# Far sums one group later on TensorE, and GpSimd's gathers with one wait a group

## The reference

```python
h = maximum(layernorm(x), 0)
# per edge: 8 radial functions of the distance -> two layers of 64 with silu -> 128 weights
weight = silu(silu(rbf @ fc_w1 / sqrt(8)) @ fc_w2 / 8) @ fc_w3 / 8
gs, gv = lin1(h)[src]                      # 32 scalars and 32 vectors of each edge's source node
msg_s = [w00 * gs * sh0, w11 * (gv . sh1) / sqrt(3)]
msg_v = [w01 * gs x sh1, w10 * gv * sh0]
agg = segment_sum(msg, dst) / clip(count, 1)
out = x + sc(h) + tanh(agg_s @ alpha_w) * lin2(agg)
```

## Time and profile before

| | us |
|---|---|
| median of 3 runs | 2496.71 |
| lowest, highest | 2487.68, 2497.35 |
| span of the profiled execution | 2483.8 |
| busy: TensorE, VectorE, GpSimd, ScalarE | 1811.4, 1783.0, 1578.4, 1199.1 |

### The profile page before, as it was taken

How to read it: one execution, slowest core, us unless ns; L and a number is a source line. 1 busy time by engine, 2 the same in 40 slices (tenths; PEclk the granted TensorE clock), 3 DMA queues, 4 the chain that set the end, 5 groups by cost and what they waited for, 6 DMA issues and landing times. The chain is left out here.

```text
span 2483.8 us, 34021 instructions
## 1 busy us (share of the span) xinstructions
PE 1811.4 (73%) x7969; PEld 1174.2 (47%) x7969; DVE 1783.0 (72%) x4669; ACT 1199.1 (48%) x3310; POOL 1578.4 (64%) x1624
## 2 busy tenths in 40 slices
PE   6577777787777777767677767667787776877777
PEld 6344444454444444444444434444554444544544
DVE  8577767767776777767676667767677776777777
ACT  6354545455454555444444344445444444445443
POOL 7566666666666666666666666666666666666563
PEclk9588878878888887788787878888888888888889
DMA  7322222222222222222122222222222222222222
GB/s 214 70 64 67 56 64 66 66 56 66 66 59 62 67 65 56 55 48 50 46 50 48 48 48 49 54 50 64 57 67 62 59 65 66 53 64 61 59 66 55
DMA packets 347699, 155.73 MB, mean 63 GB/s; under 512 B 237983, under 2 KB 322048, under 8 KB 347584
## 3 DMA queue, kind: packets, MB, share of 16 engines
q0 software_dynamic: 50016, 102.51, 15.7%
q1 hardware_dynamic: 296938, 51.75, 11.4%
q10 hardware_dynamic: 630, 0.29, 0.0%
HBM read 134.27 MB, written 20.15 MB: 62 GB/s over the span
## 5 line engine op out<-in xcount | busy, mean ns | idle before, releaser
L970 POOL DMA_INDIRECT lin_g<-lin_table,src_ix x1563 | 1530.0, 979 | 865.1 <-issue 441.5
L1157 ACT ACTIVATE lin_sh<-lin_g,harm 128x128 f32<-128x128 f32 x1563 | 483.8, 396 | 94.6 <-DMA lin_g<-lin_table,src_ix 87.6
L1040 PE MATMUL ps_sums<-near_sums,far_hot 128*128 128x257 f32 x520 | 208.0, 488 | 440.8 <-DVE agg L1474 206.0
L1030 PE MATMUL ps_near<-msg,onehot 128*64 128x257 f32 x3126 | 507.5, 471 | 1.2 <-DVE msg L1423 1.2
L1018 PE MATMUL ps_w<-w,h 128*128 128x256 f32 x1566 | 462.6, 440 | 28.2 <-ACT key_all L1167 18.5
L1018 PEld LDWEIGHTS ps_w<-w,h 128*128 128x128 f32 x1566 | 395.3, 272 | 135.4 <-issue 44.9
L999 PE MATMUL ps_h<-rbf,w 32*128 32x192 f32 x1044 | 277.0, 390 | 138.0 <-issue 67.1
L1415 DVE TENSOR_TENSOR msg<-lin_sh,key_all 128x576 f32<-128x576 f32 (+1 forms) x261 | 197.3, 756 | 249.9 <-ACT key_all L1167 209.5
L1167 ACT ACTIVATE key_all<-ps_w 128x768 f32<-128x768 f32 x261 | 213.5, 818 | 305.2 <-remote 188.6
L1030 PEld LDWEIGHTS ps_near<-msg,onehot 128*64 128x64 f32 x3126 | 241.3, 164 | 230.6 <-issue 175.7
L1383 DVE TENSOR_TENSOR lin_sh<-lin_g,ps_meta 128x576 f32<-128x576 f32 (+1 forms) x261 | 196.6, 753 | 212.2 <-DMA lin_g<-lin_table,src_ix 207.0
(11 more groups left out here) (175 smaller groups left out, 1655.2 us busy)
## 6 DMA issues: line engine op xcount, KB each, us to landing
lin_g<-lin_table,src_ix POOLq DMA_INDIRECT x1563
dist_in<-in_edge_weight SPq DMA_DIRECT2D x67, 96.0 KB
lin_table<-lin_out SPq DMA_DIRECT2D x24, 256.0 KB, 2.6
x_in<-in_x SPq DMA_DIRECT2D x24, 256.0 KB
skip_table<-x_in SPq DMA_DIRECT2D x24, 256.0 KB
xq<-in_x SPq DMA_DIRECT2D x23, 256.0 KB, 3.9
harm<-in_edge_attr SPq DMA_DIRECT2D x66, 48.0 KB
x_in<-skip_table SPq DMA_DIRECT2D x8, 256.0 KB
```

The costliest lines, as they stand in the source:

```text
L970: pool.indirect_dma_start(slot_tiles(s, u)[rows, t, :], None, lin_table, bass.IndirectOffsetOnAxis(ap=src_ix[rows, s.phase, u, col:col + 1 ...
L1030: mm = pe.matmul(ps_near[half * NEAR:(half + 1) * NEAR, 0:MSG + 1], onehot[:, u, t, :], msg[:, u % 2, t, :], start=(j == 0), stop=(j == PA ...
L1040: pe.matmul(ps_nodes(i), far_hot[:, u, :], near_sums[:, u % 2, :], start=True, stop=True).then_inc(sums_ready, 1)
L1157: last = act.activation(lin_sh0[:, u % 2, j, :], slot_tiles(s, u)[:, j, :], ACT.Copy, scale=harm[:, s.phase, u, harm_col(j):harm_col(j) + 1])
```

## The change

The far sum moves one group back and up: in slot g TensorE computes that of g-2, between the first and the second layer. VectorE's aggregation of g-2 stands between the product and the one-hot columns. The near sums always wait for ScalarE's copy of the sums before, since no far sum does it for them any more. `turn_early` (transposes of blocks of `agg` that are complete) waits for the aggregation of the last group of the iteration before. GpSimd keeps the wait ahead of a group's first gather and loses the two others.

```diff
@@ gather (GpSimd)
                             for k, t in enumerate(tiles):
-                                if not first and k == 2:
-                                    pool.wait_ge(h2_done, s.i * SLOTS + u)
-                                    pool.nop(nofuse=True)
-                                if not first and k == 4:
-                                    pool.wait_ge(sums_ready, s.i * SLOTS + u - SLOTS + 1)
-                                    pool.nop(nofuse=True)
@@ near_layer (TensorE)
                             pe.wait_ge(msg_ready, n + 1)
-                            if isinstance(i, int) and i == ITERS:
-                                pe.wait_ge(near_copied, n)
+                            at_least(pe, near_copied, n)
@@ turn_early (TensorE)
+                            if k == 0:
+                                pe.wait_ge(agg_ready, (EARLY0 + n) * SLOTS + 1)
@@ body (TensorE)
                                     layer1(i, u + 3)
+                                if u > 1:
+                                    segment_sum(i, u - 2)
+                                elif not isinstance(i, int) or i > 0:
+                                    segment_sum(i - 1, SLOTS - 2 + u)
                                 if not last or u + 2 <= SLOTS:
                                     layer2(i, u + 2)
                                 layer3(i, u + 1)
-                                if u > 0:
-                                    segment_sum(i, u - 1)
-                                elif not isinstance(i, int) or i > 0:
-                                    segment_sum(i - 1, SLOTS - 1)
                                 near_layer(i, u)
...
                         body(ITERS - 1, finish=True, last=True)
+                        segment_sum(ITERS - 1, SLOTS - 2)
                         segment_sum(ITERS - 1, SLOTS - 1)
@@ body (VectorE)
                             for u in range(SLOTS):
+                                if not last or u < SLOTS - 1:
+                                    products(s, u + 2)
                                 if u > 1:
                                     accumulate(i, u - 2)
                                 elif not isinstance(i, int) or i > 0:
                                     accumulate(i - 1, SLOTS - 2 + u)
                                 if not last or u < SLOTS - 1:
-                                    products(s, u + 2)
                                     columns(s, u + 2)
                                 late(s, u + 1)
```

## The result

The changed kernel takes 2580.11 us (median of 4 runs, 2561.38 to 2594.81), the kernel before 2496.42 beside it (2487.68 to 2497.35): 1.0335 times before, 95% interval 1.0285 to 1.0386. It is slower, and lies above the forecast of 2446 us and above the range of 2290 to 2570. It went as rival C had it in kind.

What follows compares the result with a forecast made beforehand. GpSimd's gathers and the gaps between them were taken as the bound: span 2483.8 - 66 (GpSimd) + 10 (TensorE) + 5 (new waits) + 0 (VectorE) = 2433 us, plus 12.9 gives 2446 us; range 2290 to 2570.

Steps and rivals of the forecast that it cites:

- rival C: GpSimd's removed pauses had kept news flowing: slower above 189 head pauses, 2542 us mostly, up to 2646; 30%.
- Step 1: GpSimd's two waits go: 154 head pauses of 1.9 us, 293 us against 359, saving 66 us.
- Step 2: TensorE's far sum moved: earlier near sums, nothing added; layers two and three later, 10 us lost (bounds 0 to 80).
- Step 3: TensorE's new waits: near sums for ScalarE's copy, zero; early transposes for the aggregation, 5 us (0 to 117).
- Step 4: VectorE's aggregation behind the product: register load hidden, up to 188 us back, or 110 us lost; taken as 0.
- A: GpSimd's wait at the head of a group rarely stops: 72 pauses left, 2258 us; 12%.
- B: Late news through ScalarE's copy, VectorE's message and the near sums sets the pace: no change, 2497 us; 13%.

Runs made afterwards that it cites:

- the memset: Kernel before without GpSimd's waits ahead of the third and fifth gather, plus a memset of 1000 values ahead of each group's fourth gather: 2515.24 us, 1.0084.
- the plain loads: Kernel before without GpSimd's waits ahead of the third and fifth gather, its gathers replaced by SyncE loading the same bytes from fixed rows: 2155.93 us, 0.8652.
- sum_late_only: Kernel before, all three GpSimd waits kept, with only TensorE's new order; VectorE's aggregation stays at the head of its slot: 2558.27 us, 1.0259.
- aggregation_late_only: Kernel before with only VectorE's aggregation moved behind the product; TensorE's order and GpSimd's three waits unchanged: 2547.57 us, 1.0074.
- gates_off_old_order: Kernel before with only GpSimd's waits ahead of the third and fifth gather removed: 2577.83 us in the one execution that counts, 1.021.

## Why the prediction was wrong

**The diagnosis was right in the main.** GpSimd's gathers and their gaps set the pace, and late completions mostly come through when it stops issuing. That was inferred from order; the memset and the plain loads show it. That a recorded matmul end is an estimate does not account for the 9 us, since such ends were right to 0.03 us with GpSimd silent. The prediction's own rows also show that news comes through beside unbroken gathers (1316.93) and that a stop of 1.71 us can leave it unsaid; it did not use this.

**Step 1, GpSimd, failed, in one term.** It forecast 154 pauses at the head and 1.9 us of excess for each, 293 us. Measured were 156 pauses with 3.21 - 0.30 = 2.91 us, 454 us: 161 above the forecast and 95 above the 359 of before. The 1.9 came from the mean of all pauses (1.66) and a little more, with the cap of 3.2 - 0.3 that "remote" pauses showed. I read those pauses as short because a gate had let news through shortly before. Pauses at the head are of another kind: after 6 gathers in a row the late news includes what the near sums themselves needed, so that TensorE is truly behind ("PE ps_near" 263.0 us in 61, longest 13.6; before 15.9 in 13; with a break added to the changed kernel 88.3 in 40). The step took the length from a state that the change removes. It said that silence would leave more unsaid, and priced this at 0.24 us.

**Step 2, TensorE.** Half right. The sum's wait of 440.4 us went (92.6 left); whether earlier near sums gain anything no run took apart. The price taken, 10 us out of 0 to 80, was beside the point: the cost of the late sum is that VectorE waits for it (501 us in `sum_late_only`), not layers two and three behind it.

**Step 3, the new waits.** Not on any path: TensorE ahead of the near sums waits 21.4 us in 21 for ScalarE's copy, and the transposes wait for the aggregation once, 2.9 us, where 5 were taken. Right.

**Step 4, VectorE.** Taken 0, with bounds of -188 and +110. The register load's gap went in part (188.0 to 76.0), but the aggregations, forecast almost without idle time before them, have 319.7 us of it (190.7 before), as they wait for the far sum instead. And the move costs 0.74% in `aggregation_late_only`, by a term the step had not: gathers that last longer, 27 us in the changed kernel.

**The rivals.** C was right in kind, with its decision point misplaced: it asked for 189 pauses of 1.9 us, and the loss came with 156 longer ones. It should have been stated in us of excess (359), not as a number of pauses at a fixed length. A is out (156 pauses, not 72). B, no change, is out too, by the interval. The weights gave C 0.30 although its mechanism was the one that the forecast's own reading of the trace implied; that a pause releases the news and that removing pauses is harmless could not both be true at one price.

Closing the sum with measured terms: 2483.8 + 95 (excess) - 18 (60 pauses became plain gaps, at 0.30 each 18 us more, yet the plain gaps came to 441.6 us as against 441.5) + 27 (gathers) + 5 = 2593, the span of the changed kernel.

**What stays open.** Why completions are late while GpSimd issues, why some come through all the same, and whether it is the indirect kind of transfer, GpSimd's writing of it, or the queue that counts; what the gates alone are worth, between 2 and 4%; whether a break longer than 1.11 us would do still better; and how much of the moves' 1.5% is the longer gathers.

## What to carry to other kernels

A wait on the pacing engine can be what lets the others run: before taking it out, look at what is released during it and how soon after, and price the next wait by what will have piled up, not by the mean of today's. Replace a suspect wait by idle work of the same length, and by none: the two runs tell what it orders from what it gives. A recorded TensorE end isn't the moment at which others hear of it; where "remote" ends the waits behind a matmul, ask what GpSimd was issuing.

## What the runs showed of the hardware

**Completions of TensorE are told late while GpSimd issues indirect transfers back to back.** 12.8 us in the stretch of after, 0.03 us with GpSimd silent and SyncE loading the same bytes. Three came 1.0, 1.4 and 2.0 us after the last gather before a break had ended. Others came beside unbroken gathers, 3.8 us late at 1316.93 before and 12.8 us late at 1331.79 after. With a gap of 0.37 us twice a group GpSimd still paused for 535.2 us at the head, with one of 1.11 us for 246.3.

**A gather lasts longer beside VectorE's messages.** In the stretch of after, the gather of 1324.11 takes 1.32 us where its median is 0.94, and it is the one that stands beside the operations of 1324.79 and 1325.06, with two operands each from SBUF. The whole timeline bears it out (from 100 to 2450 us in the trace of after): of 144 gathers of over 1.05 us, 141 overlap one of the message's four operations with both operands in SBUF (L1411 to L1416). The 361 gathers beside these have a mean of 1.15 us, the 1109 others 0.94, and so have the 93 beside the message's last operation alone, which reads one operand from PSUM. In `aggregation_late_only` it is 187 of 188, with means of 1.22 and 0.95, so the moved aggregation puts more of the gathers' time there. Over the span the mean of a gather was 979 ns before, 966 in `gates_off_old_order` and 1020 in `aggregation_late_only`. The Trainium skill ("GPSIMD Engine Reference", section "1. Specifications") gives GpSimd's SBUF interfaces as shared with VectorE, with contention at VectorE instructions with two SBUF inputs. The rows agree; no run here took the message away from beside the gathers to try it.
